# Fourth attention of an eight-stage network: projections as pieces inside the units, scores and exponentials in pairs of heads

## The reference, cut to what matters

```python
    q = (x @ Wq).reshape(b, s, H, 2 * D)
    k = (x @ Wk).reshape(b, s, KVH, 2 * D)
    v = (x @ Wv).reshape(b, s, KVH, D)
    q = _rope(q)
    k = _rope(k)
    ...
    energy = jnp.einsum('bqhad,bkhad->bahqk', qd, kd)
    causal = jnp.triu(jnp.ones((s, s), dtype=bool), 1)
    energy = jnp.where(causal, NEG, energy)
    scores = jax.nn.softmax(energy / np.sqrt(D), axis=-1)
    lam = (jnp.exp(jnp.sum(lq1 * lk1, -1)) - jnp.exp(jnp.sum(lq2 * lk2, -1)) + LAM_INIT)[None, :, None, None]
    diff = scores[:, 0] - lam * scores[:, 1]
    diff = jnp.where(causal, NEG, diff)
    diff = jax.nn.softmax(diff, axis=-1)
    att = jnp.einsum('bhqv,bvhd->bqhd', diff, v)
    att = att * jax.lax.rsqrt(jnp.mean(att * att, axis=-1, keepdims=True) + EPS) * rms_w
    att = att * (1.0 - LAM_INIT)
    return att.reshape(b, s, E) @ Wo
```

## Time and profile before

| | us |
|---|---|
| median of 3 runs | 3110.26 (3109.85 to 3111.97) |
| the profiled execution | 3111.67 |
| its span in the profile | 3109.9 |
| PE busy in the span | 2608.6 (84%) |
| DVE busy | 1858.5 (60%) |
| ACT busy | 1310.5 (42%) |
| POOL busy | 359.7 (12%) |
| mean granted clock of TensorE | 0.917 |

### The profile page before, as it was taken

How to read it: one execution, slowest core, us unless ns; L and a number is a source line. 1 busy time by engine, 2 the same in 40 slices (tenths; PEclk the granted TensorE clock), 3 DMA queues, 4 the chain that set the end, 5 groups by cost and what they waited for, 6 DMA issues and landing times. The chain is left out here.

```text
span 3109.9 us, 43072 instructions
## 1 busy us (share of the span) xinstructions
PE 2608.6 (84%) x14256; PEld 1883.3 (61%) x14256; DVE 1858.5 (60%) x4295; ACT 1310.5 (42%) x3605; POOL 359.7 (12%) x392
## 2 busy tenths in 40 slices
PE   7988999889999999998698877796555654999997
PEld 5665544457776777677476665543443433877876
DVE  3665233445464555445645757546888886777777
ACT  4663455533443344334222132205777773332322
POOL 2440000000000000000121000003444440000000
PEclk9998999989999999999899888896777776999998
DMA  3002000000000000002000000100000003000000
GB/s 148 10 7 82 1 0 0 0 35 1 3 3 3 0 3 3 3 0 75 16 0 0 0 0 0 37 6 29 24 19 19 24 9 132 1 1 0 0 0 27
DMA packets 26415, 56.11 MB, mean 18 GB/s; under 512 B 3696, under 2 KB 22896, under 8 KB 24688
## 3 DMA queue, kind: packets, MB, share of 16 engines
q1 hardware_dynamic: 26352, 55.32, 4.8%
HBM read 39.59 MB, written 2.10 MB: 13 GB/s over the span
## 5 line engine op out<-in xcount | busy, mean ns | idle before, releaser
L1864 ACT ACTIVATE l3a_pr<-psum,l3a_nm 128x128 f32<-128x128 f32 (+1 forms) x512 | 207.1, 430 | 202.8 <-DVE l3a_nm L1961 202.8
L1721 PE MATMUL psum<-l3a_kr,l3a_qr 32*128 32x128 f32 (+1 forms) x1024 | 91.1, 491 | 180.3 <-ACT l3a_pr L1864 176.9
L108 DVE TENSOR_TENSOR x_sb<-psum,x_sb 128x512 f32 (+2 forms) x48 | 41.7, 868 | 235.2 <-PE psum L950 135.5
L757 DVE TENSOR_TENSOR l0f_hg<-l0f_sq,psum 128x512 f32<-128x512 f32 x128 | 87.8, 688 | 151.1 <-ACT l0f_sq L689 148.3
L1721 PEld LDWEIGHTS psum<-l3a_kr,l3a_qr 32*128 32x128 f32 x1024 | 51.5, 271 | 198.8 <-ACT l3a_pr L1864 186.3
L995 ACT ACTIVATE l1a_pr<-psum,l1a_nb,l1a_rq 128x128 f32<-128x128 f32 (+1 forms) x256 | 127.2, 509 | 87.2 <-DVE l1a_nb L1048 84.9
L1221 POOL TENSOR_TENSOR l1f_acc<-l1f_t 128x512 f32<-128x512 f32 x4 | 6.3, 1573 | 1334.3 <-DVE l1f_t L1284 1334.3
L2178 PE MATMUL psum<-l3f_x_hi,l3f_w_hi 128*128 x384 | 154.5, 402 | 6.6 <-DVE l3f_w_lo L2261 6.6
L2225 ACT ACTIVATE l3f_sg<-psum 128x512 f32<-128x512 f32 x96 | 57.3, 597 | 240.3 <-PE psum L2181 240.3
L1961 DVE TENSOR_REDUCE l3a_nm<-psum 128x2 f32<-128x256 f32 (+1 forms) x256 | 124.6, 548 | 53.9 <-PE psum L1725 53.9
L2179 PE MATMUL psum<-xT,l3f_w_hi 128*128 x384 | 152.9, 398 | 0.0
(11 more groups left out here) (424 smaller groups left out, 6942.2 us busy)
## 6 DMA issues: line engine op xcount, KB each, us to landing
w_l3f_all<-l3f_all_dram SPq DMA_DIRECT2D x1, 9216.0 KB, 25.7
l3a_qr<-l3a_q_all SPq DMA_DIRECT2D x32, 256.0 KB, 2.5
w_l0f_w<-l0f_w_dram SPq DMA_DIRECT2D x2, 2048.0 KB, 10.0
w_l1f_all<-l1f_all_dram SPq DMA_DIRECT2D x1, 2560.0 KB, 8.8
x_sb<-x_dram SPq DMA_DIRECT2D x1, 2048.0 KB, 8.5
l0a_xc<-xT SPq DMA_DIRECT2D x8, 256.0 KB, 2.5
w_l1a_q<-l1a_q_dram SPq DMA_DIRECT2D x1, 2048.0 KB, 7.9
w_l1a_k<-l1a_k_dram SPq DMA_DIRECT2D x1, 2048.0 KB, 13.5
```

Source lines behind the costliest of these rows:

```text
L1721: mm(S[:, g, t * P:t * P + (t + 1) * P], qr[rows, a, r, t * P:(t + 1) * P], kr[rows, a, 0:(t + 1) * P], start=(t == 0), stop=False, tile_p ...
L1864: last = nc.scalar.activation(pr[:, r, a, g, k], S[:, g, k], ACT.Exp, bias=nm[:, i % 2, g, t:t + 1], accum_out=sums[:, r, a, g, t:t + 1])
```

## The change

It rewrites `l3_attention` (line numbers of the kernel before; the diff is cut to its core).

1. **Projections as pieces.** `q_all`, the keys in `xT` and the values of all batches are gone. Seven pieces per batch (keys of both maps, four of queries, values) stand inside the units: in units 1, 2, 3, 5, 6 of batch b the pieces of batch b + 1, in unit 0 the last queries and in unit 4 the values of b itself. A piece is eight matmul records on 256 columns into bank 6 or 7 (`OT`, `OB`), which also carry the values' output and its transpose. DVE takes a piece in the same unit (`piece_in`). SyncE copies only one slice of x per batch (`xc`). Five pieces stand ahead of the first scores.
2. **Pairs.** `scores`, `maxima` and `exponentials` run on one pair of heads at a time (two PSUM banks); the scores of a pair wait only for that pair's exponentials of the unit before.
3. **Order.** TensorE: scores of pair 0, values (even units), transposes into bank 4, scores of pair 1, the piece, transposes into bank 5, transpose back (even). All lags grow by one unit.
4. **Differences.** All on GpSimd, for two heads at a time; DVE's `difference` is gone.
5. **Norm.** `take_output` copies the output with its row sum as it is (`raw`, 17 columns per head) instead of dividing; the division is folded into the normalisation. It moves from unit 5 to unit 6.

```diff
-        q_all = sb("q_all", [P, A, R, TOK])
+        xc = sb("xc", [P, KD, T])
...
+                def project_queries(b, r, dst):
+                    for a in range(A):
+                        for k in range(KD):
+                            last = mm(dst[:, a * T:(a + 1) * T], w["q"][:, k, (a * R + r) * P:(a * R + r + 1) * P], xT[:, k, bass.ds(b * T, T)],
+                                      start=(k == 0), stop=(k == KD - 1))
+                    last.then_inc(piece_ps, 1)
...
+                def scores(b, i, pair, opening):
...
                     if not (opening and i == 0):
-                        pe.wait_ge(p_exp, b * NU + i)
+                        pe.wait_ge(p_exp, 2 * (b * NU + i) - 1 + pair)
...
+                def turn(b, i, j):
+                    s = b * NU + i - 4
+                    r, heads = (i - 4) // 2 % R, part(i - 4)
+                    if j == 0:
+                        pe.wait_ge(p_ready, s + 1)
+                    pe.wait_ge((pt_even, pt_odd)[j], s + 1)
...
                     for i in range(NU):
+                        turning = live(i, 4, opening, closing)
+                        done = i % 2 == 0 and live(i, 6, opening, closing)
                         if not closing:
-                            scores(b, i, opening)
...
+                            scores(b, i, 0, opening)
+                        if done:
...
                             values(b, i)
+                        if turning:
+                            turn(b, i, 0)
+                        if not closing:
+                            scores(b, i, 1, opening)
+                            piece(b, i, opening, more)
+                        if i == 7 and not opening:
+                            turn_output(b - 1)
+                        if turning:
+                            turn(b, i, 1)
+                        if done:
...
+                            turn_back(b, i)
                         if i == 7 and not opening:
                             if not closing:
                                 pe.wait_ge(on_raw, b * R + 1)
                             project_output(b - 1)
...
                     for t in range(TT):
                         k = slice(t * P, t * P + (t + 1) * P)
-                        last = nc.gpsimd.tensor_tensor(pr[:, r, 1, g, k], pr[:, r, 1, g, k], ratio[:, r, g, t:t + 1].broadcast_to((P, (t + 1) * P)), ALU.mult)
+                        last = nc.gpsimd.tensor_tensor(pr[:, r, 1, heads, k], pr[:, r, 1, heads, k], bc(ratio[:, r, heads, t], 2, (t + 1) * P), ALU.mult)
                     last.then_inc(scaled, 1)
                     pool.wait_ge(scaled, s + 1)
-                    nc.gpsimd.tensor_tensor(pr[:, r, 0, g, :], pr[:, r, 0, g, :], pr[:, r, 1, g, :], ALU.add).then_inc(dif_odd, 1)
+                    nc.gpsimd.tensor_tensor(pr[:, r, 0, heads, :], pr[:, r, 0, heads, :], pr[:, r, 1, heads, :], ALU.add).then_inc(dif_ready, 1)
...
                         if not closing:
-                            exponentials(b, i, opening)
+                            exponentials(b, i, 0, opening)
+                        if i == 7 and not opening:
+                            output(b - 1)
+                        if not closing:
+                            exponentials(b, i, 1, opening)
+                        if live(i, 4, opening, closing):
+                            out_of_psum(b, i, opening)
...
                             second(b, i)
...
                     for i in range(NU):
                         if not closing:
-                            maxima(b, i)
...
+                            maxima(b, i, 0)
+                        if i % 2 == 0 and live(i, 1, opening, closing):
+                            ratios(b, i)
+                        if i % 2 == 0 and live(i, 6, opening, closing):
+                            values_out(b, i)
+                        if i % 2 == 1 and live(i, 7, opening, closing):
...
+                            take_output(b, i)
+                        if not closing:
+                            maxima(b, i, 1)
+                            if i == 7 and more:
+                                add_keys(b * NQ + 8)
+                            if i < 7:
+                                piece_in(b, i, more)
+                        if live(i, 4, opening, closing):
+                            out_of_psum(b, i, opening)
+                        if live(i, 3, opening, closing):
                             second_maxima(b, i)
...
                         if not opening:
-                            if i == 5:
+                            if i == 6:
                                 norm_1(b - 1)
                                 norm_2(b - 1)
```

More of the change, by code:

```diff
@@ new lines, in turn @@
+                def turn(b, i, j):
[4 more added lines that the diff above has]
+                    pe.wait_ge((pt_even, pt_odd)[j], s + 1)
+                    for k in range(3):
+                        last = nc.tensor.transpose(PT[j][:, k * P:(k + 1) * P], pr[:, r, 1, heads.start + j, k * P:(k + 1) * P], c["id"])
+                    last.then_inc(pt_ps, 1)
@@ L1819, in difference @@
                     s = b * NU + i
-                    r, g = i // 2, part(i).start + 1
+                    r, heads = i // 2, part(i)
                     if i % 2 == 0:
@@ L1853, in _, with exponentials @@
                 act.sem_inc(pt_even, 1)
-                def exponentials(b, i, opening):
+                def exponentials(b, i, pair, opening):
                     r, a = i // A, i % A
-                    if not opening:
+                    if pair == 0 and not opening:
                         act.wait_ge(pt_ps, b * NU * 2 + 4 * r - 12)
-                    for g in range(G):
-                        if g % 2 == 0:
-                            act.wait_ge(nm_ready, b * NU * 2 + 2 * i + g // 2 + 1)
+                    act.wait_ge(nm_ready, 2 * (b * NU + i) + pair + 1)
+                    for g in range(2 * pair, 2 * pair + 2):
                         for t in range(TT):
@@ L1866, in exponentials, with out_of_psum @@
                     last.then_inc(p_exp, 1)
-                def out_of_psum(b, i):
-                    s = b * NU + i - 3
-                    r, g = (i - 3) // 2 % R, part(i - 3).start
+                def out_of_psum(b, i, opening):
+                    s = b * NU + i - 4
+                    r, g = (i - 4) // 2 % R, part(i - 4).start
+                    if not (opening and i - 4 < 4):
+                        act.wait_ge(av_ps, b * R + (i - 4) // 2 - 1)
                     act.wait_ge(pt_ps, 2 * s + 1)
@@ L1965, in ratios, with maxima @@
+                def maxima(b, i, pair):
+                    dve.wait_ge(s_ps, 2 * (b * NU + i) + pair + 1)
+                    for t in range(TT):
+                        last = nc.vector.tensor_reduce(nm[:, i % 2, 2 * pair:2 * pair + 2, t],
+                                                       S[:, 2 * pair:2 * pair + 2, t * P:t * P + (t + 1) * P], AX.X, ALU.max, negate=True)
+                    last.then_inc(nm_ready, 1)
                 def ratios(b, i):
-                    r = i // 2
```

349 lines of the change are left out of this document (162 added, 187 removed).

## The result

The changed kernel takes 3190.26 us (3187.66 to 3194.32), the one before 3111.11 (3109.85 to 3113.69) in the same session: a ratio of 1.0254, 95% interval 1.0237 to 1.0272. I had forecast 3148 us, 38 more than before; it is 79 more, and 0.3 us above my range. The direction and the mechanism were right, the sum was too small.

What follows compares the result with a forecast made beforehand. No engine was full; a ring of waits between engines bound the units. Front -82, batch 0 -1, six batches +111, batch 7 +8, drain +2: net +38, 3148 us; range 3065 to 3190, the forecast's own 3120 to 3170.

Steps and rivals of the forecast that it cites:

- The front: First projection to first scores, 92.9 us before: five pieces, a rotation and the keys' sum remain; gain 81.6 us.
- Rival (d): Front: setup or a weight's DMA holds the first scores, 10 us more; chance called small, no number given.
- The ring and its gate: Units: transposes wait for the previous unit's second exponentials, ahead of second pair's scores and piece; 7.47 us warm, 9.5 forecast.
- Rival (b): Units: the split pays, bias and piece hide, units near 6.3 us, 55 per batch, 3010 in all; chance 0.06.
- Scores and masks of a pair 0.8 (cold 1.4): Units, on TensorE: scores and masks of two heads take 0.8 us at full clock, 1.4 at the low level.
- The clock: Units: TensorE idles 2.3 us or more, so the work after starts at the low level; 9.5 us instead of 7.47.
- Rival (a): Units: the pieces keep TensorE warm, 60 to 67 us per batch, 3050 to 3090 in all; chance 0.27.
- Rival (c): Units: piece always at low level, bias behind the mask each time; 80 to 82 per batch, about 3180; chance 0.15.
- The port: Even units: DVE's two-operand bias waits for the end of GpSimd's instruction; unit 9.3 or 11.5 us, taken as 10.4.
- Batch 0: 51 to 52, as before: First batch, no second half in its first units: 51 to 52 us against 52.5 before, -1.
- Batch 7 and the drain: Last batch with two pieces 66 us, +8; drain with both differences on GpSimd in a row, +2.
- End of a batch: Units 6 and 7: normalisation waits for the mask's end, then maxima, exponentials and output, 22 us; unit 0 then 6.5.

Runs made afterwards that it cites:

- the last version: Changed kernel with each unit's scores together, transposes behind the piece, output's copy late and normalisation behind unit 7's maxima: 3042.68 us, 0.9783 of before.

## Why the prediction was wrong, and where it was right

- **The front**: right. 10.46 us to the first scores, 11.3 forecast; the five pieces and the sum of the keys are the chain. Rival (d), no gain in the front, fell.
- **The ring and its gate**: right. TensorE idles 1.96 and 3.45 us before the transposes in the turns shown, ended by the second exponentials; moving them gave 118 us. Rival (b), the split pays, fell with the three runs that made the scores together or split them alone.
- **"Scores and masks of a pair 0.8 (cold 1.4)"**: this term failed. I took it between half of four heads' price and a little more (the half of 0.87 and 0.5 is 0.69, not 0.66). It is 1.09 and 1.99, since a pair's scores take as long as four heads' (0.92 for 8 records, 0.94 for 16): 0.29 and 0.59 too little. The run without the masks shows that this place pays in full on the average (0.41 us per unit). Of the 42 us missed 19 lie in batches 1 to 6, 10 in batch 0 and 13 in batch 7 and the drain. In batches 1 to 6 the term makes some 9 by the odd units (three of 0.5 in each batch) and the longer piece some 5; in even units that wait for GpSimd both are hidden.
- **The clock**: right in kind (0.74 to 0.77), too mild in size. After all thirteen waits of 2.7 us and more the three transposes began at the low level (0.90 in most), after those of 1.2 to 2.6 at either (0.55 or 0.90). The change of level that I put 4.4 us behind a cold start gave a piece of 3.1 us; in the odd units it took 3.45 on the mean. With idle matmuls the clock was 0.91 and 54.8 us were won. Rival (a), pieces that keep TensorE warm, fell. Rival (c), "cold and masked", came near in number (80 to 82 per batch and 3180 or a little over; 79.5 and 3190 measured) and held only in part: 12 of 43 pieces ran warm, and in 10 of the 32 even units the bias took more than 1 us.
- **The port**: right in kind. The bias takes 0.16 us in the odd unit shown and 1.83 in the even one, to the end of GpSimd's mask, and 12.6 us went with the mask. The Trainium skill, page "SBUF — State Buffer", section "SBUF: two separate sides", calls it an exclusive lock; the rows agree for two tensor operands in SBUF. My own numbers had the bias due at 7.4, behind the mask's start at 7.2, so they gave 11.5 us and not the mean of 9.3 and 11.5. That unit 2 took 10.9 comes from a faster GpSimd: a difference took 3.46 us (2350.80 to 2354.26) where I had 3.75, its sum 1.80 and not 2.05. All waits of the bias together are 24 us over 0.16 us each; what the move of all differences to GpSimd costs was not tested by itself.
- **"Batch 0: 51 to 52, as before"**: this step failed too. The first four units, without a second half, took 18.7 us (2030.69 to 2049.39). From there each unit is a full turn of the ring, whose price I had left out: 42.9 us to the first scores of batch 1 (2092.31). Its first turn, TensorE after:

```profile
2049.39 0.92 PE L1749 MATMUL psum<-l3a_kr,l3a_qr 32*128 32x128 f32 x8
2050.24 0.40 PE L1753 MATMUL psum<-cb_sb 128*128 128x128 bf16 x4
2054.85 0.90 PE L1763 MATMUL psum<-cf_sb,l3a_pr 128*128 128x128 f32 x3 [4.21 <-ACT l3a_pr L1920]
2055.68 1.65 PE L1749 MATMUL psum<-l3a_kr,l3a_qr 32*128 32x128 f32 x8
```
- **Batch 7 and the drain**: too small by 13 us. The units without a piece take 7.9 to 8.4 us there between second exponentials; I had 6.3, the sum with warm transposes and 0.8 for the pair, so the failed term is here too. With 0.83 and 1.99 it is 0.05 + 0.83 + 1.99 + 0.13 + 1.06 + 1.59 + 0.37 + 1.89 = 7.9. What the drain adds I didn't test by itself.
- **End of a batch**: 22 us for units 6 and 7 was too much and 6.5 for unit 0 too little (19.3 and 9.9 on the mean of batches 1 to 6, by second exponentials); these errors nearly cancel, which is luck. Two slips stand beside them: the squares take 1.09 us per batch, not 2.2, which is in no sum, and in the 22 us 9.55 and 3.8 make 13.4, not 12.7.

## What to carry to other kernels

When an operation is split so that its first half may start earlier, look at what the queue puts between the halves: a wait there gates everything behind it, and moving three transposes past the piece was worth 118 us. Price the halves by what runs side by side in the array, since half of the heads in half of the row groups takes the whole time. In the last version a batch takes what it took before (58.1 us), with the same projections in its units, and of the front's 82 us a gain of 68 is left. That version also moves the normalisation, which the kernel before wasn't given, so the price of the pieces by themselves isn't shown.

## What the runs showed of the hardware

- Eight scores' records in two row groups take 0.92 us, sixteen in four groups 0.94 (1.65 and 1.66 at the low level): a row group has four records in both, and the time goes by them, not by the number of groups.
- DVE's instructions with a per-partition scalar, or with one tensor operand, didn't wait for GpSimd (0.58 us for four, 0.18 for one of 32 elements while GpSimd ran), while those with two tensor operands in SBUF did, 1.68 and 2.26 us instead of 0.19.
- In the kernel before with its scores split, TensorE was busy 339 us in 400 and its granted clock was 0.63; with idle matmuls in the changed kernel it was busy 342 and the clock 0.91. Busy time in the trace doesn't tell the clock: the slower it is, the longer the same work counts as busy.
